# Decoder layer on one core: tiles, scores and transposed halves of the attention stage in another order

## The reference

```python
x = _layernorm(x + gated_mlp(x, w_gate, w_up, w_down))          # half of the gate values set to 0
q = rmsnorm(x @ Wq.T, q_norm_w)                                 # 32 heads of 128, 4 x 256 queries
k = rmsnorm(ctx @ Wk.T, k_norm_w)                               # 8 key heads of 128, 4 x 1601 keys
v = ctx @ Wv.T
probs = softmax(q @ k.T / sqrt(128) + mask)                     # 4 query heads share a key head
x = _layernorm(x + (probs @ v) @ Wo.T)
x = _layernorm(x + experts(x, route_w, A, Bw))                  # one of 8 low-rank experts per row
```

## Time and profile before

| | |
|---|---|
| median of 3 runs | 2526.08 us (2525.43 to 2528.13) |
| profiled execution, its own time | 2523.99 us |
| its span | 2522.2 us |
| busy PE / DVE / ACT / POOL | 2389.3 / 1846.0 / 1612.7 / 1399.5 us |
| attention's first and last `take_o` | at 1013.3 and 2317.5 us |
| chain that ended last | PE 65%, DVE 10%, issue 9%, DMA 7%, ACT 4%, SP's queue 3% |

### The profile page before, as it was taken

How to read it: one execution, slowest core, us unless ns; L and a number is a source line. 1 busy time by engine, 2 the same in 40 slices (tenths; PEclk the granted TensorE clock), 3 DMA queues, 4 the chain that set the end, 5 groups by cost and what they waited for, 6 DMA issues and landing times.

```text
span 2522.2 us, 44822 instructions
## 1 busy us (share of the span) xinstructions
PE 2389.3 (95%) x12414; PEld 1644.2 (65%) x12414; DVE 1846.0 (73%) x2769; ACT 1612.7 (64%) x3248; POOL 1399.5 (55%) x1239
## 2 busy tenths in 40 slices
PE   9999999999999996999999999999999999998999
PEld 8878888888888874555555555555555555555887
DVE  5899999995774354777777777777777777775544
ACT  3178777786634555777777777777777777775321
POOL 0177777877511346666666666666666666653000
PEclk9999999999999998999999999999999999999999
DMA  6343334434453464877777777777777778777532
GB/s 229 111 128 105 112 117 125 125 105 129 157 184 111 146 203 110 177 188 174 185 175 186 171 187 175 185 175 186 170 186 171 188 176 184 173 159 210 160 110 67
DMA packets 740851, 398.29 MB, mean 158 GB/s; under 512 B 485072, under 2 KB 687952, under 8 KB 740784
## 3 DMA queue, kind: packets, MB, share of 16 engines
q1 hardware_dynamic: 740784, 397.49, 61.3%
HBM read 183.85 MB, written 96.11 MB: 111 GB/s over the span
## 4 chain that ended last, share of the span: by engine, by line
PE 65%; DVE 10%; issue 9%; DMA 7%; ACT 4%; SPq 3%; POOL 2%; DVEq 1%; ACTq 0%; POOLq 0%
PE banks L206 17%; PE banks L207 17%; PE banks L208 17%; PE banks L1137 8%; DMA pT_dma<-halves 6%; PE banks L2568 3%; DVE pT_lo L2501 3%; DVE p_odd L2464 2%; DVE p_even L2464 2%; PE banks L436 2%; ACT pT_hi L2423 1%; SPq L2181 1%; ACT k_hi L2381 1%; DVE halves L2286 1%; SPq L2130 1%
## 5 line engine op out<-in xcount | busy, mean ns | idle before, releaser
L1058 DVE TENSOR_SCALAR_CACHE_REDUCE flags<-abs_s,thr 128x1376 bf16<-128x1376 f32 x256 | 403.7, 1643 | 1.1
L206 PE MATMUL banks<-k_hi,q_hi 128*128 128x416 f16 (+1 forms) x1024 | 341.5, 333 | 11.5 <-DVE t_min L2464 9.1
L2464 DVE CUSTOM_DVE_ANT_0 p_even<-banks,minus_mask,guard_scalars 128x1664 f32<-128x1664 f32 x128 | 249.7, 1951 | 128.5 <-PE banks L208 127.1
L2464 DVE CUSTOM_DVE_ANT_0 p_odd<-banks,minus_mask,guard_scalars 128x1664 f32<-128x1664 f32 x128 | 249.7, 1951 | 128.5 <-PE banks L208 126.7
L207 PE MATMUL banks<-k_lo,q_hi 128*128 128x416 f16 (+1 forms) x1024 | 341.1, 333 | 0.0
L208 PE MATMUL banks<-k_hi,q_lo 128*128 128x416 f16 (+1 forms) x1024 | 340.9, 333 | 0.0
L2423 ACT CAST pT_hi<-banks 128x512 f16<-128x512 f32 x384 | 217.4, 585 | 185.1 <-PE banks L2568 184.0
L2501 DVE TENSOR_TENSOR pT_lo<-banks,pT_hi 128x512 f16<-128x512 f32 (+1 forms) x384 | 258.3, 687 | 45.9 <-ACT pT_hi L2423 45.9
L2396 ACT ACTIVATE p_even<-p_even,t_min 128x1601 f32<-128x1601 f32 x128 | 209.0, 1633 | 69.8 <-DVE t_min L2468 69.0
L2396 ACT ACTIVATE p_odd<-p_odd,t_min 128x1601 f32<-128x1601 f32 x128 | 208.9, 1632 | 52.9 <-DVE t_min L2468 52.1
L206 PE MATMUL banks<-pT_hi,v_hi 128*128 128x512 f16 x320 | 123.0, 384 | 91.6 <-DVE pT_lo L2501 89.1
(11 more groups left out here) (283 smaller groups left out, 6453.5 us busy)
## 6 DMA issues: line engine op xcount, KB each, us to landing
raw<-keys SPq DMA_DIRECT2D x32, 800.5 KB, 4.9
keys<-kT_sb SPq DMA_DIRECT2D x50, 512.0 KB, 4.7
values<-v_sb SPq DMA_DIRECT2D x50, 512.0 KB, 3.0
raw<-values SPq DMA_DIRECT2D x32, 768.0 KB
queries<-qT_sb SPq DMA_DIRECT2D x64, 256.0 KB, 2.6
raw<-queries SPq DMA_DIRECT2D x32, 512.0 KB, 5.3
r_sb<-query_roots SPq DMA_DIRECT2D x32, 512.0 KB, 6.7
inv_b<-inverse_sums SPq DMA_DIRECT2D x64, 256.0 KB, 3.4
```

Source lines behind the costliest of these rows:

```text
L206: pe.matmul(out, a_hi, b_hi, start=start, stop=False)
L1058: bits.done(dve.tensor_scalar(flags[:, tt % 2], abs_s[:, tt], thr[:, tt:tt + 1].bitcast(F32), 0.0, ALU.is_lt, ALU.add, accum_out=out[:, tt ...
L2464: dve.tensor_tensor_reduce(banked(p_sb[u % 2][:, j, 0:KP]), psum[:, 0:SB, 0:SW], banked(minus_mask[:, j % 2]), guards.score_scale, 3.40282 ...
```

## The change

Positions of products, transposes and scores in a unit move, with everything that hangs on them on the other engines; the transposing DMA of a row tile becomes two, one for each half; the tail of the values is split by POOL (in four instructions) and no more by DVE (in two); both mask halves are shaped by POOL; the first unit's row tiles are split and turned at earlier steps. The order by position:

| pos | 0 | 1 | 2 | 3 | 4 | 5 | 6 | 7 | 8 | 9 | 10 | 11 | 12 |
|---|---|---|---|---|---|---|---|---|---|---|---|---|---|
| before: score | 1 | | | | 2 | | | 3 | | | 0' | | |
| product | P0 | P1 | P2 | P3 | D | D | D | P4 | D | D | P5 | D | D |
| transpose | n3 | | | | n4 | | | n5 | | | n0' | n1' | n2' |
| after: score | 1 | | | 2 | | | 3 | | | 0' | | | |
| product | P0 | P1 | P2 | D | D | P3 | D | D | P4 | D | D | P5 | D |
| transpose | | | n3 | | | n4 | | | n5 | | n0' | n1' | n2' |

```diff
@@ queries, sync
+            if last_trip(i) and s - TT in (4, 5, 7):
+                attention.early["turn_halves"](sp, 0, 0, (4, 5, 7).index(s - TT))
@@ attention
-    P_AT = (0, 1, 2, 3, 7, 10)
+    P_AT = (0, 1, 2, 5, 8, 11)
-    AT = {0: 1, 4: 2, 7: 3, 10: 0}
-    TURN_AT = {0: 3, 4: 4, 7: 5, 10: 0, 11: 1, 12: 2}
+    AT = {0: 1, 3: 2, 6: 3, 9: 0}
+    TURN_AT = {2: 3, 5: 4, 8: 5, 10: 0, 11: 1, 12: 2}
@@ turn_landed
-        return landed(TT // 2 + n)
+        return landed(TT // 2 + 2 * n + 1)
@@ turn_halves
-        wait_apart(sp, (lo_dve, lo_pool)[j % 2], done_down(n), sp_passed)
-        sp.dma_start_transpose(pT_dma[u % 2][:, :, P * j:P * (j + 1)], halves[j % 2][:]).then_inc(turned[j % 2], 16)
+        for part, ready in enumerate(((hi_pool, hi_act), (lo_dve, lo_pool))):
+            wait_apart(sp, ready[j % 2], done_down(n), sp_passed)
+            sp.dma_start_transpose(pT_dma[u % 2][:, ND * part:ND * (part + 1), P * j:P * (j + 1)],
+                                   halves[j % 2][:, DW * part:DW * (part + 1)]).then_inc(turned[j % 2], 16)
@@ sync, position
-            if pos == 0:
-                store_inverse(i, u)
-            if pos == 3 and after:
+            if pos == 2 and after:
                 turn_halves(sp, i, u + 1, 0)
-            if pos == 4 and not last_trip(i):
+            if pos == 3 and not last_trip(i):
                 ... load_next_v or load_next_kq
+            if pos == 4:
+                store_inverse(i, u)
             if pos == 5 and after:
                 turn_halves(sp, i, u + 1, 1)
@@ sync, before the loop
-        for j in range(QT):
-            turn_halves(sp, 0, 0, j)
-            if j == 0:
-                load_next_v(sp, 1)
+        turn_halves(sp, 0, 0, QT - 1)
+        load_next_v(sp, 1)
@@ split_tail, now (pool, item, slot), at position 11 of even units
-            dve.scalar_tensor_tensor(at, at, low, raw, ALU.mult, ALU.add).then_inc(v_lo_done, 1)
+            pool.tensor_scalar(at, at, low, 1.0, ALU.mult, ALU.mult).then_inc(v_lo_done, 1)
+            pool.tensor_tensor(at, at, raw, ALU.add).then_inc(v_lo_done, 1)
@@ early_gpsimd
         if s == -2:
+            for r in range(S // P):
+                pool.tensor_scalar(minus_mask[:, r, 0:KV], ... -7e34, guards.mask_scale, ALU.max, ALU.mult)
-        s == 2 scale_v; 3 scale(1); 4 hi 0; 4, 5 split_body_lo; 6 lo 1, hi 2, tails 1, 2; 7 tail 3
+        s == 1 scale_v; 2 hi 0, scale(1); 3 lo 1, split_body_lo 0; 4 hi 2, split_body_lo 1;
+             6 tail 3, lo 3, split_tail
@@ gpsimd, position (hi, lo: halves of row tile j)
-            0 hi 0; 3 lo 1; 4, 7, 11 split_kq_lo; 4, 7 split_body_lo; 6 hi 2; 9 lo 3
+            0 hi 0; 1 split_kq_lo 0; 3 lo 1; 5 hi 2; 6 split_kq_lo or split_body_lo, two; 9 lo 3; 11 split_tail
@@ gpsimd, before the loop
-        halves_lo_pool(pool, 0, 0, 3)
@@ scalar, position (behind split_p)
-            exp at 0, 4, 7, 12; halves_hi_act at 0, 7; split_kq_hi at 3, 6, 9; split_v_hi at 3, 6
+            exp at 2, 5, 8, 12; halves_hi_act at 2, 8; split_kq_hi at 0 (two), 3; split_v_hi at 3, 6
@@ vector, position
-            0 invert; subtract_mask at AT; split_p at TURN_AT; halves_lo_dve at 0, 7; 12 split_tail
+            subtract_mask at AT; 3 invert; halves_lo_dve at 0, 6; then split_p at TURN_AT
```

More of the change, by code:

```diff
@@ L2108, in columns @@
         return slice(0, P), slice(a, b)
-    KQ = [split(q_raw, q_hi, q_lo, columns(0, 2 * QW)), keys(slice(0, SB // 2)), keys(slice(SB // 2, SB))]
+    KQ = [keys(slice(0, SB // 2)), keys(slice(SB // 2, SB)), split(q_raw, q_hi, q_lo, columns(0, 2 * QW))]
     V = [split(v_raw, v_hi, v_lo, columns(0, NT * HD // 2)), split(v_raw, v_hi, v_lo, columns(NT * HD // 2, NT * HD))]
@@ L2328, in early_gpsimd @@
             repeat_tail(pool, 0, 0, 0)
-        if s in (4, 5):
-            split_body_lo(pool, 0, 0, s - 4)
-        if s == 6:
[L2332 to L2336, removed]
+            scale(pool, 1)
+        if s == 3:
+            halves_lo_pool(pool, 0, 0, 1)
+            repeat_tail(pool, 0, 0, 1)
+            split_body_lo(pool, 0, 0, 0)
+        if s == 4:
+            halves_hi_pool(pool, 0, 0, 2)
+            repeat_tail(pool, 0, 0, 2)
+            split_body_lo(pool, 0, 0, 1)
+        if s == 6:
             repeat_tail(pool, 0, 0, 3)
+            halves_lo_pool(pool, 0, 0, 3)
+            split_tail(pool, 0, 0)
     def gpsimd(pool):
@@ L2351, in position @@
                 repeat_tail(pool, i, u + 1, 1)
[L2352 to L2356, removed]
+            if pos == 5 and after:
                 halves_hi_pool(pool, i, u + 1, 2)
                 repeat_tail(pool, i, u + 1, 2)
-            if pos == 7 and splits_kq(i, u):
+            if pos == 6 and splits_kq(i, u):
+                split_kq_lo(pool, *kq_item(i, u), 2)
                 split_kq_lo(pool, *kq_item(i, u), 1)
-            if pos == 7 and splits_v(i, u):
+            if pos == 6 and splits_v(i, u):
+                split_body_lo(pool, *v_item(i, u), 0)
                 split_body_lo(pool, *v_item(i, u), 1)
@@ L2411, in early_scalar @@
             halves_hi_act(act, 0, 0, 1)
+        if s in (3, 4):
+            split_v_hi(act, 0, 0, s - 3)
+        if s == 6:
+            halves_hi_act(act, 0, 0, 3)
         if s == 7:
@@ L2432, in position @@
                 split_p(i, *turn(u, pos))
-            if pos in (0, 4, 7) and after:
-                exp(act, i, *scored(u, pos))
+            if pos in (2, 5, 8) and after:
+                exp(act, i, u + 1, TURN_AT[pos] - 2)
             if pos == NT - 1 and exists(i, u + 2):
                 exp(act, i, u + 2, 0)
-            if pos in (0, 7) and after:
-                halves_hi_act(act, i, u + 1, AT[pos])
+            if pos in (2, 8) and after:
+                halves_hi_act(act, i, u + 1, TURN_AT[pos] - 2)
+            if pos == 0 and splits_kq(i, u):
+                split_kq_hi(act, *kq_item(i, u), 0)
+                split_kq_hi(act, *kq_item(i, u), 1)
             if pos == 3 and splits_kq(i, u):
-                split_kq_hi(act, *kq_item(i, u), 0)
+                split_kq_hi(act, *kq_item(i, u), 2)
             if pos == 3 and splits_v(i, u):
                 split_v_hi(act, *v_item(i, u), 0)
-            if pos == 6 and splits_kq(i, u):
-                split_kq_hi(act, *kq_item(i, u), 1)
             if pos == 6 and splits_v(i, u):
                 split_v_hi(act, *v_item(i, u), 1)
-            if pos == 9 and splits_kq(i, u):
-                split_kq_hi(act, *kq_item(i, u), 2)
             if last_unit(i, u) and pos == 5:
@@ L2487, in early_vector @@
             dve.wait_ge(pads, 7)
+        if s == 4:
+            halves_lo_dve(dve, 0, 0, 0)
         if 1 < s <= 5:
@@ L2490, in early_vector @@
         if s == 6:
[L2491 to L2492 removed]
+            halves_lo_dve(dve, 0, 0, 2)
         if s == 7:
@@ L2520, in position @@
             after = exists(i, u + 1)
-            if pos == 0:
-                invert(i, u)
             if pos == NT - 1:
@@ L2526, in position @@
                 subtract_mask(dve, i, *scored(u, pos))
+            if pos == 3:
+                invert(i, u)
+            if pos in (0, 6) and after:
+                halves_lo_dve(dve, i, u + 1, 0 if pos == 0 else 2)
             if pos in TURN_AT and exists(i, turn(u, pos)[0]):
                 split_p(i, *turn(u, pos))
-            if pos in (0, 7) and after:
-                halves_lo_dve(dve, i, u + 1, 0 if pos == 0 else 2)
-            if pos == NT - 1 and splits_v(i, u):
-                split_tail(dve, *v_item(i, u))
-        halves_lo_dve(dve, 0, 0, 2)
         for n in range(3):
@@ L2623, in attention @@
     return Stage(sync, gpsimd, scalar, vector, tensor, {
-        "open": open_counts, "rows": rows, "first_loads": first_loads, "first_v": lambda sp: load_v(sp, 0), "last_v": last_v,
+        "open": open_counts, "rows": rows, "turn_halves": turn_halves, "first_loads": first_loads, "first_v": lambda sp: load_v(sp, 0), "last_v": last_v,
         "second_kq": lambda sp: load_next_kq(sp, 1), "last_exp": lambda act: exp(act, 0, 0, QT - 1), "gpsimd": early_gpsimd,
```

42 lines of the change are left out of this document (18 added, 24 removed).

## The result

The changed kernel takes 2499.85 us (median of 4 runs, 2498.12 to 2505.49), the kernel before beside it 2525.76 (4 runs, 2525.00 to 2528.13): ratio 0.990, 95% interval 0.9883 to 0.9917. It is 26 us faster where 74 were forecast. The profiled execution took 2498.12 us, its span 2496.3.

What follows compares the result with a forecast made beforehand. PE was taken as the bound, 95% busy, with gains only from its waits. 62 units at 1.04 us less (64.5) plus 10 at the start make 74.5 us off, 2451.6 on the median; range 2428 to 2503.

Steps and rivals of the forecast that it cites:

- P3: Steady unit: PE's wait of 1.46 us before product P3 goes, with 1.6 us to spare.
- Scores: Steady unit: three scores 4.43 us apart cost PE nothing; any DVE delay ahead would be PE's one to one.
- The wait moves: Rival, chance 0.10: the saved wait returns before a score or at P4, DVE lacking room; only the start gains, 2516.
- `n0'` and the exp: Steady unit: transpose n0' waits 0.69 us for ACT's exp of row tile 3 instead of 0.27, plus 0.42.
- The wait at P3: Steady unit: PE's wait for DVE's `pT_lo` before product P3, 1.46 us a unit, goes.
- The two DMAs: SP: eight transposing DMAs a unit instead of four, each half taking 0.95 us to issue; fits.
- turning point: SP's issue time for a half, 1.45 us, above which SP bounds and the kernel turns slower; that rival's chance 0.08.
- the sum of SP's unit: SP's issuing per steady unit: 8 x (0.95 + 0.25) plus 7.3 for other DMAs, 16.9 of 19.5 us.
- The split DMA does nothing: Rival: SP reaches the second half late anyway; time as forecast, its chance included in the forecast's 0.60.
- a later second landing: Rival, chance 0.18: halves queue, the low half lands up to 1.9 us later, costing 28 us: 2480.
- The start: Before the steady units: POOL's path 8 us sooner, PE's wait at first output minus 2; 10 us, bounds 3 and 14.
- 41.3 + 7.2 + 1.4: Start: POOL's busy time, second mask half and four small instructions, 49.9 us without waits, to 985.8, 8.9 sooner.

Runs made afterwards that it cites:

- the last experiment: Changed kernel with POOL waiting for DVE's low half at positions 1 and 6, ACT's exp of row tile 3 first, and one transposing DMA: 2426.18 us, ratio 0.9614.
- the one with both edits: Changed kernel with POOL waiting for DVE's low half at positions 1 and 6 and ACT's exp of row tile 3 first, two transposing DMAs: 2444.16 us, ratio 0.9685.

## Why the prediction was right or wrong

**The size of `halves_lo` was the step that failed.** In "P3" the forecast had DVE's operations between n3 and P3 end by 6.1, with `halves_lo` at the 1.13 us of the earlier trace rows; in "Scores" it stood at nothing. That row was measured where POOL's scaling of the values, begun at 1410.91 and 1.65 long, had 0.2 us left to run. The new order puts DVE's half at the end of score 1 of position 0 and POOL's scaling at position 1, 0.6 us ahead of it, and the half took 2.70 and 1.98 us. The price in the odd unit was 0.36 at P3 and 0.77 at the score, in the even 0.29: mean (0.36 + 0.77 + 0.29) / 2 = 0.71 of the 20.44 - 19.72 = 0.72 that the period was off. The sentence "if DVE has something ahead of it, that delay is PE's one to one" was right; nothing had been put there. Stopping the meeting gave 2456, and a period of 19.71. The room was smaller than the forecast had it, too: it let `subtract_mask` start at about 2.1 in the unit, but the earlier trace rows have it at 1409.53 - 1406.92 = 2.61, and with POOL waiting it starts at 2.38 and P3's `pT_lo` ends 1.3 us ahead of P3 instead of 1.6. That alone would have cost nothing.

The trace of before held a hint: the 96 halves of the 1000 us took from 1.08 to 1.44 us with the same shape and no wait, and the two longest (at 1474.64 and 1972.88) started while POOL's scaling ran. The new order takes `split_p` from between `subtract_mask` and the half, which brings DVE forward into POOL's instruction. The Trainium skill says in "SBUF — State Buffer", section "SBUF: two separate sides", that DVE and GpSimd share a pair of ports by an exclusive lock, taken by a DVE operation with two SBUF inputs against a GpSimd operation that reads SBUF, for the whole instruction. The trace agrees: 1.6 us blocked and 1.09 of its own, and a `k_lo` blocked in turn, while `pT_lo` and `subtract_mask`, which read one of their inputs from PSUM, keep 0.68 and 1.94 us. The forecast did not weigh that rule.

**"The wait moves"** was a rival with 0.10 and 2516. It named the place, a score, and DVE's want of room as the cause. Half of it came true: the wait came back there, at 0.77 and 0.29 instead of all of it, by another mechanism. DVE had its room, as the forecast said against that rival, though less than its 4.9 us: DVE's 752 us in 1000 are 15.6 a unit, which leaves 4.1 of 19.7.

**`n0'` and the exp.** 0.69 forecast, 0.69 and 0.70 seen. The chain on ACT that it was read from was left alone by the change.

**The wait at P3.** 1.46 forecast to go; 2.4 us in 49 units are left in the list (by starts 0.36 in the odd unit above), and they go with the collision.

**The two DMAs.** Issuing a half takes 1.23 us, forecast 0.95, and turning point 1.45; so SP was not the bound. They land in 3.0 us from the issue instead of 4.0 for the whole:

```profile
L2184 SPq DMA_TRANSPOSE pT_dma<-halves x512: 1220/1232/3747, 956.1 to 2278.1; - x171
...
DMA to landing us min/median/max: 2.9/3.0/8.1
```

At 1.23 the sum of SP's unit is 8 x (1.23 + 0.25) + 7.3 = 19.1, above the forecast's 16.9, and just under 19.72. "The split DMA does nothing" held in the new order at either period (2501 against 2500, 2458 against 2456), and "a later second landing" did not come at 20.4 or 19.7 us. At 19.5 the second DMA cost 18 us, as the last experiment shows against the one with both edits; whether by a later landing or by SP's issuing is open.

**The start.** 10 forecast, 11.9 seen, in part by luck: POOL's first high half came 11.3 sooner where 8 was taken, and the rest of the way to the first output gave 0.6 where 2 was. That high half, of unit 1, is at 983.34 (forecast 986). The row of the two mask halves shows 6.6 us each for the 7.21 of the earlier trace rows; the first score's `subtract_mask` waits 4.95 us for them, PE 3.55 in turn:

```profile
932.77 13.19 POOL L2326 TENSOR_SCALAR minus_mask<-minus_mask,guard_scalars 128x1601 f32<-128x1601 f32 x2
...
983.34 0.94 POOL L2284 TENSOR_SCALAR halves<-p_odd 128x896 f16<-128x896 f32 x1
```

That wait was not priced. POOL is busy nearly all of that stretch (50.12 of 52 us), so the 41.3 + 7.2 + 1.4 of the forecast hold it already. The four small instructions took 0.37, 0.37, 0.43 and 0.43, in sum 1.6 for 1.4.

**Not priced: the last trip.** 3 us are lost between the 61st output and the 62nd, 24.15 us where 21.41 were before. ACT stands 3.17 us ahead of a cast of the output weights that waits for its load, and POOL's low half behind it. In the kernel before the same cast, at 2276.16, had no wait. After:

```profile
2249.83 1.04 ACT L2787 CAST wo_hi<-raw 128x1024 fp32r<-128x1024 f32 x1 [3.17 <-DMA raw<-WoT_in]
```

That this is the cause of the 3 us is argued from the rows, not tried.

## What to carry to other kernels

A duration belongs to the company in which it was measured. When an order of work moves, list for each DVE instruction with two SBUF inputs what POOL runs at the moment it will start, and price the meeting at what is left of POOL's instruction, if DVE is on the path there (at position 6 it was not); a wait that lets the cheaper engine go second (here POOL, which lost up to 2 us and needed none of it) was worth 43 us here. And when a stall is taken away, try earlier edits again: a second DMA that was free at 20.4 us a unit cost 18 us in all at 19.5.

## What was not expected of the hardware

Half the columns of a transposing DMA is not half the issue: 1.53 us for 1792 and 1.23 for 896 in the median, so by an estimate 0.93 of it doesn't depend on size, if the two are on one line. The Trainium skill says that generations before the newest push a command for each tile of a transpose ("DMA: Bandwidth & Descriptors", "Why a DMA increments its semaphore by 16 and not by 1"); in proportion that would be an estimate of 0.77 for the half. The trace agrees that the issue grows, but by 0.30 and not by 0.77. The mask's instruction of POOL, a maximum and a product over 128x1601, takes 6.6 us, where the scaling of the values, two products over 128x1664 and over a smaller tile, takes 2.00 for both. And six transposes took SP 13.62 us behind three loads and the inverse's load, which themselves took 0.33 to 0.40 us to issue; the worst of the earlier trace rows was 5.68 for one.
